# Chunk places of the edge build packed two words to a group and unpacked by TensorE's register operations

## The reference

```python
W = zeros((1024, 1024)).at[dst, src].add(edge_weight)      # entries outside of W are dropped
h = maximum(layernorm(x), 0)
x = x + h @ W.T + L0_bias
h = maximum(layernorm(x), 0)
A = edges as an adjacency matrix (counts), deg = its row sums
for (W_self, W_neigh, b), relu in the two layers:
    h = h @ W_self + (A @ h / max(deg, 1)) @ W_neigh + b   # relu behind the first
x = x + h
```

## Time and profile before

| | us |
|---|---|
| median of three runs (lowest, highest) | 808.79 (808.02, 810.63) |
| the profiled execution | 807.12 |
| its span in the trace | 805.1 |
| granted TensorE clock, mean | 0.995 |
| TensorE busy | 771.7 |
| VectorE, ScalarE, GpSimd busy | 484.8, 370.6, 409.7 |

### The profile page before, as it was taken

How to read it: one execution, slowest core, us unless ns; L and a number is a source line. 1 busy time by engine, 2 the same in 40 slices (tenths; PEclk the granted TensorE clock), 3 DMA queues, 4 the chain that set the end, 5 groups by cost and what they waited for, 6 DMA issues and landing times.

```text
span 805.1 us, 13264 instructions
## 1 busy us (share of the span) xinstructions
PE 771.7 (96%) x4548; PEld 638.7 (79%) x4549; DVE 484.8 (60%) x718; ACT 370.6 (46%) x526; POOL 409.7 (51%) x570
## 2 busy tenths in 40 slices
PE   4778999999999999999999999999999999999998
PEld 3767788888888888788878878888888888878786
DVE  6999477778454788867413543136568766245443
ACT  6866634334264232223246876453222223348663
POOL 5000167667659888765742210127898747724310
PEclk9999999999999999999999999999999999999999
DMA  3112456775566753577855643566735669668654
GB/s 111 41 64 86 136 178 194 234 249 183 181 221 202 271 170 110 175 232 277 274 181 187 210 142 105 171 215 232 256 123 168 210 198 324 223 202 270 219 157 141
DMA packets 83127, 151.40 MB, mean 188 GB/s; under 512 B 10965, under 2 KB 21068, under 8 KB 83056
## 3 DMA queue, kind: packets, MB, share of 16 engines
q1 hardware_dynamic: 61534, 102.65, 40.6%
q10 hardware_dynamic: 20002, 42.91, 14.9%
q0 software_dynamic: 1520, 4.92, 1.5%
HBM read 103.79 MB, written 46.65 MB: 187 GB/s over the span
## 4 chain that ended last, share of the span: by engine, by line
PE 74%; DVE 8%; POOL 8%; issue 4%; ACT 3%; DMA 2%; POOLq 0%; ACTq 0%; SPq 0%; DVEq 0%
PE bank L1435 37%; PE bank L1477 19%; PE bank L1370 13%; DVE L L1655 3%; POOL split L920 2%; DVE R L1640 2%; POOL T L937 2%; DVE L L1647 1%; ACT Ax L1145 1%; PE bank L1282 1%; POOL T L935 1%; PE bank L1493 1%; PE bank L1266 1%; PE bank L1363 1%; POOL S L902 1%
## 5 line engine op out<-in xcount | busy, mean ns | idle before, releaser
L1435 PE MATMUL bank<-slot,split 128*128 128x512 f32 x1680 | 386.5, 391 | 0.6 <-POOL split L920 0.6
L1435 PEld LDWEIGHTS bank<-slot,split 128*128 128x128 f32 x1680 | 313.6, 188 | 66.7 <-issue 2.3
L882 POOL TENSOR_TENSOR AT<-AT,az 128x50 int32 (+3 forms) x288 | 95.9, 333 | 117.6 <-DMA az<-asum_scratch 76.8
L920 POOL TENSOR_TENSOR split<-stage,split 128x512 fp32r<-128x512 f32 x50 | 65.9, 1320 | 117.7 <-ACT split L1113 117.6
L1145 ACT CAST Ax<-AT 128x1280 fp32r<-128x1280 uint16 x40 | 106.9, 2680 | 35.3 <-PE bank L1477 19.6
L1790 DVE TENSOR_TENSOR slot<-T,slot 128x512 fp32r<-128x512 f32 x64 | 87.8, 1400 | 21.7 <-ACT slot L1104 20.5
L1370 PE MATMUL bank<-slot,split_m 128*128 128x512 f32 x320 | 91.2, 396 | 0.0
L1113 ACT CAST split<-stage 128x512 fp32r<-128x512 f32 x50 | 31.2, 624 | 119.3 <-PE bank L1435 69.5
L1477 PE MATMUL bank<-slot,Ax 128*128 128x512 f32 x320 | 77.2, 393 | 0.6 <-ACT Ax L1145 0.6
L1790 DVE TENSOR_TENSOR slot<-wst,slot 128x512 fp32r<-128x512 f32 x48 | 47.2, 1009 | 49.2 <-ACT slot L1104 49.2
L1910 DVE SCALAR_TENSOR_TENSOR cst<-bank,dinv,stage 128x512 f32<-128x512 f32 x40 | 30.0, 751 | 73.6 <-PE bank L1477 73.1
(11 more groups left out here) (193 smaller groups left out, 1064.9 us busy)
## 6 DMA issues: line engine op xcount, KB each, us to landing
stage<-hT_scratch SPq DMA_DIRECT2D x90, 256.0 KB, 3.6
wst<-in_L_gnn_W_neigh SPq DMA_DIRECT2D x56, 256.0 KB, 4.9
wst<-in_L_gnn_W_self SPq DMA_DIRECT2D x56, 256.0 KB, 3.0
x1b_scratch<-x ACTq DMA_DIRECT2D x10, 512.0 KB, 5.8
hT_scratch<-hTs ACTq DMA_DIRECT2D x10, 512.0 KB, 3.1
stage<-prod0s_scratch SPq DMA_DIRECT2D x20, 256.0 KB, 3.0
hT_scratch<-h1s ACTq DMA_DIRECT2D x20, 256.0 KB, 3.5
stage<-prod1s_scratch SPq DMA_DIRECT2D x20, 256.0 KB, 3.0
```

Source lines behind the costliest of these rows:

```text
L882: pool.tensor_tensor(a, a, az32[:, n % NZ, pairs * pos:pairs * (pos + 1)], ALU.add) \
L920: pool.tensor_tensor(split[:, v % 2, 1, :], source(v), split[:, v % 2, 0, :].bitcast(F32), ALU.subtract).then_inc(s_olo, 1)
L1435: last = pe.matmul(dense_bank(v, which)[:, :], split[:, v % 2, a, NT * k:NT * (k + 1)], slot[t % 2][:, b, HF * (HK * which + k):HF * (HK * ...
```

## The change

1. **The table.** `tab_g` now has three integers a group: four places of 6 bits each (without the factor 8) in each of two words, and the base. `shift` becomes `pairs` (second of two x 64 + first) and then words (second pair x 4096 + first pair): two operations of VectorE instead of one. SyncE brings the whole table with one DMA; `tab_w` is gone.
2. **TensorE's loads.** `LOADED` says ahead of which groups words and bases are loaded: 0 (for 4 groups), 4, 12, 20 (8 each) and 28 (9), three values a group, in a row. 18 loads become 5.
3. **TensorE's register operations.** `unpacked(j)`, ahead of each group and ahead of its wait for R and L, makes the places by shifts and masks in registers: in a group of eight single chunks 6 REGISTER_ALU and 6 fused register instructions; 8 in groups 3 to 5, and 2 to 4 in groups 0 to 2. The product's place is given in steps of TW columns (`by_place`), so the address instruction of each chunk holds three operations instead of two.
4. **ScalarE's loads** of bases pick every third value of `tab_o`, 16 at a time as before.
5. **Range bases.** VectorE spreads `first` over a diagonal (`firsts_d`, 40 x 320), and one fp32r product with `tens`, now filled with TN, takes the place of the eight.

```diff
+LOADED = {0: range(0, 4), 4: range(4, 12), 12: range(12, 20), 20: range(20, 28), 28: range(28, LATE)}
...
             sp.wait_ge(s_tab, 1)
-            sp.dma_start(tab_o[:, :], tab_g[:, OFFW:OFFW + GC]).then_inc(s_tabo, 16)
+            sp.wait_ge(s_tabg, 1)
+            sp.dma_start(tab_o[:, :], tab_g[:, :]).then_inc(s_tabo, 16)
             sp.wait_ge(s_tabg, 2)
-            sp.dma_start(tab_w[:, :], tab_g[:, BASEW:BASEW + 1]).then_inc(s_tabw, 16)
...
                 if j % LOADS == 0:
-                    bases = load(act, tab_w[0:1, j:min(j + LOADS, LATE)], 0, F)
+                    bases = load(act, tab_o[0:1, COLS * j + WORDS:COLS * min(j + LOADS, LATE):COLS], 0, F)
...
-            for c in range(GC):
-                last = pe.matmul(firsts_of_edges()[:, :, c], first[:, c:c + 1].to_broadcast([NG, EP]), tens[:, :],
-                                 start=True, stop=True)
-            last.then_inc(s_span, 1)
+            pe.wait_ge(s_spans, 1)
+            pe.matmul(bank[6][0:EP, 0:NG * GC], tens[:, :], firsts_d[:, :, :].rearrange("p b c -> p (b c)"),
+                      start=True, stop=True).then_inc(s_span, 1)
...
-                        last = pe.matmul(w_bank(j)[:, bass.ds(offsets[c // SHARED[j]], kw(j))], row,
-                                         L[:, q, c, ka(j) + kw(j) * part:ka(j) + kw(j) * (part + 1)],
+                        last = pe.matmul(by_place(w_bank(j))[:, bass.ds(offsets[c // SHARED[j]], WDS[j]), :], row,
+                                         by_place(L[:, q, c, ka(j) + kw(j) * part:ka(j) + kw(j) * (part + 1)]),
...
+            def load_words(j):
+                words = load(pe, tab_o[0:1, COLS * LOADED[j].start:COLS * LOADED[j].stop], 0, 2 ** (DIGIT * DIGITS) - 1)
+                for n in LOADED[j]:
+                    words_of[n] = words[COLS * (n - j):COLS * (n - j) + WORDS]
+                    base_of[n] = nc.s_assert_within(words[COLS * (n - j) + WORDS], 0, F,
+                                                    skip_runtime_bounds_check_because=clamped)
+            def unpacked(j):
+                offsets = []
+                for c in range(0, GC, SHARED[j]):
+                    word, at = words_of[j][c // DIGITS], c % DIGITS
+                    if at > 0:
+                        pe.reg_alu(place_in_w[c], word, DIGIT * at, ALU.logical_shift_right)
+                    if at == 0:
+                        pe.reg_alu(place_in_w[c], word, 2 ** DIGIT - 1, ALU.bitwise_and)
+                    elif at < DIGITS - 1:
+                        pe.reg_alu(place_in_w[c], place_in_w[c], 2 ** DIGIT - 1, ALU.bitwise_and)
+                    offsets.append(nc.s_assert_within(nc.snap(place_in_w[c], engines=bass.OrderedEngineSet([pe.engine])),
+                                                      0, WW - WD, skip_runtime_bounds_check_because=clamped))
+                return offsets
...
-                if j not in offsets_of:
-                    load_offsets(j)
-                if j in BASES:
-                    if j == 3:
-                        pe.wait_ge(s_tabw, 16)
-                    base_of.update(zip(BASES[j], load(pe, tab_w[0:1, BASES[j].start:BASES[j].stop], 0, F)))
-                offsets = offsets_of[j]
+                if j in LOADED:
+                    load_words(j)
+                offsets = unpacked(j)
                 pe.wait_ge(s_R, j + 1)
...
-            link(dve.tensor_scalar(shift[:, :], first[:, :], base_w[:, 0:1], float(WW - WD), ALU.subtract, ALU.min))
-            dve.tensor_scalar(tab_g[:, OFFW:OFFW + GC], shift[:, :], float(TW), None, ALU.mult).then_inc(s_tab, 1)
+            shifted = tick(dve.tensor_scalar(shift[:, :], first[:, :], base_w[:, 0:1], float(WW - WD), ALU.subtract, ALU.min))
+            dve.scalar_tensor_tensor(out=firsts_d[:, :, :], in0=ident[0:NG, 0:NG].unsqueeze(2).to_broadcast([NG, NG, GC]),
+                                     scalar=1.0, in1=first[:, :].unsqueeze(1).to_broadcast([NG, NG, GC]),
+                                     op0=ALU.mult, op1=ALU.mult).then_inc(s_spans, 1)
+            dve.wait_ge(s_dve, shifted)
+            of_pair = shift[:, :].rearrange("p (n t) -> p n t", t=2)
+            link(dve.scalar_tensor_tensor(out=pairs[:, :], in0=of_pair[:, :, 1], scalar=float(2 ** DIGIT),
+                                          in1=of_pair[:, :, 0], op0=ALU.mult, op1=ALU.add))
+            of_word = pairs[:, :].rearrange("p (n t) -> p n t", t=2)
+            dve.scalar_tensor_tensor(out=tab_g[:, 0:WORDS], in0=of_word[:, :, 1], scalar=float(4 ** DIGIT),
+                                     in1=of_word[:, :, 0], op0=ALU.mult, op1=ALU.add).then_inc(s_tab, 1)
```

More of the change, by code:

```diff
@@ L50 @@
 NV = 4
-OFFW, BASEW, COLS = 0, 8, 12
+WORDS, DIGIT, DIGITS = 2, 6, 4
+COLS = WORDS + 1
 LOADS = 16
@@ L54 @@
 FIRST = 8
-AT_ONCE = 24
-BASES = {3: range(4, 8), 8: range(8, 16), 15: range(16, 32), 31: range(32, LATE)}
+LOADED = {0: range(0, 4), 4: range(4, 12), 12: range(12, 20), 20: range(20, 28), 28: range(28, LATE)}
 TURN_STATS = 8
 OV = WD
-NCONST = 14
+NCONST = 13
 NLATER = 3 * len(set(WDS)) + 1
@@ L156, in build_program @@
         tab = sb("tab", [1, NG, GC], I32, build)
-        tab_w = sb("tab_w", [1, NG], I32, build)
-        tab_o = sb("tab_o", [1, NG * GC], I32, build)
+        tab_o = sb("tab_o", [1, NG * COLS], I32, build)
         more = sb("more", [1, NG, 2], I32, build)
@@ L178, in build_program @@
         tab_g = sb("tab_g", [NG, COLS], I32, build)
-        tens = sb("tens", [NG, NG], F32, build)
+        tens = sb("tens", [NG, EP], F32R, build)
+        firsts_d = sb("firsts_d", [NG, NG, GC], F32R, build)
+        pairs = sb("pairs", [NG, GC // 2], F32, build)
         furthest = sb("furthest", [EP, NG], F32, build)
@@ L359, in build_program @@
         s_tabo = sem("s_tabo")
-        s_tabw = sem("s_tabw")
+        s_spans = sem("s_spans")
         s_wp = sem("s_wp")
@@ L540, in w_bank, with by_place @@
             return bank[4 + SET_OF[j] % 2]
+        def by_place(sums):
+            return sums.rearrange("p (d s) -> p d s", s=TW)
         def by_tile(whole):
@@ L806, in _ @@
             pool.memset(ident[:, :], 0.0).then_inc(s_const, 1)
-            pool.memset(tens[:, :], 0.0).then_inc(s_const, 1)
+            pool.memset(tens[:, :].bitcast(F32), float(TN)).then_inc(s_const, 1)
             pool.memset(ones[:, :], 1.0).then_inc(s_const, 1)
@@ L818, in _ @@
                                pattern=[[-1, P]], channel_multiplier=1).then_inc(s_const, 1)
-            pool.affine_select(out=tens[:, :], in_=tens[:, :], compare_op=ALU.not_equal, fill=float(TN), base=0,
-                               pattern=[[-1, NG]], channel_multiplier=1).then_inc(s_const, 1)
             for n, at_least in enumerate((ALU.is_ge, ALU.is_gt)):
@@ L823, in _ @@
                                    base=0, pattern=[[1, NG]], channel_multiplier=-1).then_inc(s_const, 1)
-            pool.wait_ge(s_const, 9)
+            pool.wait_ge(s_const, 8)
             for a, b in SETS:
@@ L1033, in _ @@
             act.wait_ge(s_low, 2)
-            act.copy(tab_g[:, BASEW:COLS], base_w[:, :].to_broadcast([NG, COLS - BASEW])).then_inc(s_tabg, 1)
+            act.copy(tab_g[:, WORDS:COLS], base_w[:, :]).then_inc(s_tabg, 1)
             act.activation(tab_ag[:, :], first[:, :], ACT.Copy, scale=float(TN // 2)).then_inc(s_tabg, 1)
@@ L1047, in _ @@
             act.wait_ge(s_const, NCONST)
-            act.wait_ge(s_tabw, 16)
+            act.wait_ge(s_tabo, 16)
             for j in range(LATE):
@@ L1245, in _ @@
             pe.matmul(bank[7][0:NG, 0:NG], ones[:, 0:NG], base_d[:, :], start=True, stop=True).then_inc(s_based, 1)
-            pe.wait_ge(s_low, 2)
-            for c in range(GC):
-                last = pe.matmul(firsts_of_edges()[:, :, c], first[:, c:c + 1].to_broadcast([NG, EP]), tens[:, :],
-                                 start=True, stop=True)
-            last.then_inc(s_span, 1)
+            pe.wait_ge(s_spans, 1)
+            pe.matmul(bank[6][0:EP, 0:NG * GC], tens[:, :], firsts_d[:, :, :].rearrange("p b c -> p (b c)"),
+                      start=True, stop=True).then_inc(s_span, 1)
             def column_sums(j):
@@ L1296, in spread_mean @@
                 pe.matmul(mean_bank(i), all_ones[:, :], mean[:, i % 2, :], start=True, stop=True).then_inc(s_t0, 1)
-            offsets_of, base_of = {}, {}
-            def load_offsets(j):
-                each = GC // SHARED[j]
-                upto = j + 1
-                while upto < LATE and SHARED[upto] == SHARED[j] and each * (upto + 1 - j) <= AT_ONCE:
-                    upto += 1
-                values = load(pe, tab_o[0:1, GC * j:GC * upto:SHARED[j]], 0, (WW - WD) * TW)
-                offsets_of.update((n, values[each * (n - j):each * (n - j + 1)]) for n in range(j, upto))
+            words_of, base_of = {}, {}
+            place_in_w = [pe.alloc_register(f"place_in_w{c}") for c in range(GC)]
+            def load_words(j):
[17 more added lines that the diff above has]
```

(3 more changed lines are left out.)

## The result

The changed kernel takes 834.99 us (median of four runs, 834.31 to 836.08) against 809.2 (808.02 to 810.63, four runs): a ratio of 1.032, interval 1.030 to 1.034, 25.8 us slower. The forecast was 825.4, and the range ended at 834.0: right sign, too small, and the time lies just above the range. It is the time of the rival that was given 0.05, dear registers (833 to 835).

What follows compares the result with a forecast made beforehand. TensorE's sequencer was taken to bound the build stage: 22.2 + 72.5 + 2.4 + 6.2 + 2.2 = 105.5 us against 88.9, +16.6 us, so 825.4 us on the median of 808.79; range 810 to 834.

Steps and rivals of the forecast that it cites:

- dear registers: Rival, TensorE's sequencer: 0.115 us a register instruction, and halved clock in wide groups; +24 to +26 us, chance 0.05.
- Where the time is lost: Build stage: TensorE's sequencer (loads, register instructions, waits) is the bound; moving the first transposition of W moves the end equally.
- Price of a register instruction: TensorE's sequencer: 0.095 us each, twelve ahead of each group from 6 to 36, 1.14 us a group, hidden by nothing.
- The address instruction's third operation: Each chunk's address on TensorE: one operation more inside an instruction already counted; nothing, at most 1.2 us.
- Loads: TensorE's loads before groups 12, 20 and 28: 1.7, 2.0 and 2.3 us plus 0.2, together 6.2 us.
- ScalarE's spaced load: 16 bases with a stride take 3.8 us; TensorE's product at the end of group 17 waits, +2.2 us.
- Key and groups 3 to 5: Key at 9.85 us, 1.75 earlier; group 3 starts at 16.95; group 5 done at 22.2 against 23.3, -1.1 us.
- The clock: TensorE's array: 1.2 GHz likelier in narrow groups after the change, costing up to 2 us over seven groups.
- Cheap registers: Rival, TensorE's sequencer: 0.037 us a register instruction, stage 6 us earlier, 802.5 us; chance 0.12.
- the middle price: Rival, TensorE's sequencer: 0.05 to 0.08 us a register instruction, 809 to 820 us; chance 0.17 slower, 0.06 within 0.3%.

Runs made afterwards that it cites:

- experiment 1: Changed kernel with four more plain register instructions on TensorE ahead of each group from 6 on: 845.58 us, ratio to the kernel before 1.047.
- experiment 5: Changed kernel with ScalarE's bases in a table row of their own, loaded in a row instead of every third value: 831.35 us (one run).

## Why the prediction was wrong

- **Where the time is lost**: right. The bound was TensorE's sequencer; the build stage carries the change, and the rest of the program is passed on 1:1.
- **Price of a register instruction, the step that failed.** I had bounds of 0.037 and 0.115 us, said that the upper one was the nearest row, and then took 0.095: the record plus a gap borrowed from behind a load. The mean is 0.12 us (1.43 for twelve). For the six plain ones 0.095 was right (0.0925 by experiment 1); the six fused ones hold quotients and copies, which no row before had, and take 0.145. From group 6 to the last register instruction I had 74.9 us for 31 groups and their ends, 2.42 each. Measured: 115.6 - 22.1 = 93.5, less three loads (6.2) and the wait for ScalarE (2.0), 85.3, or 2.75 each. 31 x (1.43 - 1.14) = 9 us of the 10.4 is this term. (Behind the last register instruction I had 2.4 us to the transposition, measured 1.6; with that the terms close: 16.6 forecast, 25.9 measured.)
- **The address instruction's third operation**: priced at nothing, at most 1.2 us. The record grew from 37 to 46 ns, and the distance between starts, where the array isn't in the way, from 115 to between 124 and 129, which would be 2.2 to 3.5 us over 31 x 8; what is left of the 10.4 us is 1.4, with the sequencer's other work in it. Small, but it isn't nothing on an engine that is the bound.
- **Loads**: right. 12, 20 and 28 took 1.92, 1.62 and 2.52 us (6.2 with their gaps, forecast 6.2).
- **ScalarE's spaced load**: right, 3.52 us (forecast 3.8), and it held TensorE back by 1.9 us (experiment 5), forecast 2.2.
- **Key and groups 3 to 5**: right. Key at 9.71 (9.85; `first` came 0.16 us earlier in this run), group 3 at 16.83 (16.95), the unpacking of group 6 at 22.1 (22.2).
- **The clock**: that the lower level is likelier in narrow groups was right by the pace of groups 12 to 19. "Up to 2 us over seven groups" was counted beside the sum and didn't come: the sequencer's 2.75 us were longer than the 2.7 that the estimate gave the array. Group 28 at the lower level took 3.1 us instead of 2.75, and group 29 gave it back with 2.5. The text named one stretch at 1.2 GHz in the kernel before, 46 to 49.2 us; there is a second, from 32.2 to 35.6.
- **The rivals.** Cheap registers and the middle price: refuted by experiment 1, where even the plain ones cost 0.0925. Dear registers was the case that came true, by nearly the right price (0.115 for a mean of 0.12), and had 0.05; it said that half clock in wide groups would add to it, which it didn't, so that its time fits as well as it does is in part luck. With the nearest row as the value the sum would have been 24 us and more, and the forecast 833.

## What to carry to other kernels

Price a sequencer instruction by the distance between starts of such instructions, not by its record: the record of 32 ns stood for 92. And when bounds lie apart, take the end that the nearest row gives, with the kind of operation looked at: three operations more in an instruction, with a quotient whose result is used there (169 ns for 37), cost 0.13 us, more than a second instruction. Where loads of registers are in the way, ask first what a value costs (0.07 us in a row, 0.24 with a stride, here) against the cheapest unpacking, then move the loads under a wait that exists, and cut them so that the array doesn't run empty; that brought 7.9 us where packing lost 25.8.

## What the runs showed that I had not expected

- A fused register instruction is not one price: 37 ns for two operations (product, sum), 46 for three, 56 to 62 with a copy and a quotient, 111 with a quotient that is used again in it, 169 with five operations, 182 to 189 with six.
- In the kernel before, a load of 24 values in a row takes 1.61 to 1.64 us at three places out of ten and 1.8 to 2.1 at the others, while eight mostly take 0.59. What makes the difference stays open.
- Bringing a group forward by 1.6 us can be worth nothing on the same kernel, when the clock falls to 1.2 GHz at other places than before (0.56 of full speed from 50.0 to 53.9 us, where it was 1.00).
- By the pace of its products, the array of the changed kernel ran at 1.2 GHz through eight groups in a row, and hardly any time was lost by it, since the sequencer was slower still.
